# A masked graph attention kernel: which far blocks are turned by the vector engine, and where their mask stands

## What is computed

```
h = relu(layernorm(x))
cos = beta * (h @ h.T) / (norm2 @ norm2.T + 1e-07)
x = x + softmax(cos + (1 - adj) * -1e9, axis=1) @ h
h = relu(layernorm(x))
x = x + h @ W_self + (adj @ h / max(rowsum(adj), 1)) @ W_neigh
```

## Time and profile before

| | |
|---|---|
| median of 3 runs | 485.01 us (484.8 to 486.03) |
| profiled execution, its own time | 484.94 us |
| its span | 483.1 us |
| PE busy | 455.3 us (94%) |
| DVE, ACT, POOL busy | 294.9, 288.7, 264.0 us |
| TensorE clock granted | 1.000 |
| DMA | 59.68 MB, q1 (issued by SP) 49.42 MB |

### The profile page before, as it was taken

One profiled execution on the slowest core, in us unless ns is written; L12 is line 12 of the kernel. 1 busy time (PEld: TensorE's weight loads), 2 busy tenths in 40 slices (PEclk: granted clock), 3 DMA queues, 4 the chain that ended last, 5 costly groups with the idle time before them and its releaser, 6 DMA issues.

```text
span 483.1 us, 12207 instructions
## 1 busy us (share of the span) xinstructions
PE 455.3 (94%) x5096; PEld 380.3 (79%) x5096; DVE 294.9 (61%) x685; ACT 288.7 (60%) x437; POOL 264.0 (55%) x249
## 2 busy tenths in 40 slices
PE   0969999999999999999999998999999999999997
PEld 0837888788788887788777877887797888888886
DVE  6966656877676776768857777685776421022232
ACT  2999898767977768976797778677864000000000
POOL 3989777867958578775787578566562000000000
PEclk9999999999999999999999999999999999999999
DMA  8157879878799788997799598846500000000000
GB/s 245 28 65 153 173 141 215 196 167 163 158 232 211 156 194 148 239 208 162 137 216 222 87 203 199 188 69 98 79 3 2 6 23 20 23 23 23 23 23 22
DMA packets 45899, 59.68 MB, mean 124 GB/s; under 512 B 3600, under 2 KB 38672, under 8 KB 45840
## 3 DMA queue, kind: packets, MB, share of 16 engines
q1 hardware_dynamic: 35472, 49.42, 33.2%
q0 software_dynamic: 10368, 9.44, 24.6%
HBM read 78.25 MB, written 8.91 MB: 180 GB/s over the span
## 4 chain that ended last, share of the span: by engine, by line
PE 72%; ACT 12%; DVE 9%; issue 3%; POOL 2%; DMA 1%; SPq 0%; ACTq 0%; DVEq 0%; POOLq 0%
PE ps L1184 22%; PE ps L1058 13%; PE ps L1069 7%; ACT word L600 6%; PE ps L1167 5%; PE ps L1164 5%; PE ps L1166 5%; PE ps L1139 5%; PE ps L1142 4%; ACT ps L601 4%; PE ps L1141 4%; DVE far L866 3%; DVE word L834 1%; DVE adj_t L689 1%; DMA x_sb<-in_x_dram 1%
## 5 line engine op out<-in xcount | busy, mean ns | idle before, releaser
L453 POOL TENSOR_TENSOR near<-word,adj_t 128x1024 f32<-128x1024 f32 x72 | 151.8, 2108 | 82.9 <-DVE word L834 66.5
L600 ACT ACTIVATE word<-ps,small 128x512 f16<-128x512 f32 x144 | 136.2, 946 | 63.9 <-PE ps L1058 63.5
L834 DVE TENSOR_TENSOR word<-ps,word 128x512 f16<-128x512 f32 x144 | 105.9, 738 | 81.9 <-ACT ps L601 81.7
L1184 PE MATMUL ps<-table,adj_t 128*128 128x257 f16 x1024 | 115.0, 274 | 0.0
L1058 PE MATMUL ps<-unit_t 128*128 128x512 f16 x432 | 106.5, 379 | 6.7 <-DVE word L834 4.8
L1184 PEld LDWEIGHTS ps<-table,adj_t 128*128 128x128 fp8e4 x1024 | 100.0, 98 | 13.6
L601 ACT ACTIVATE ps<-ps,small 128x512 f32<-128x512 f32 x144 | 108.2, 751 | 0.0
L1164 PE MATMUL ps<-table,near 128*128 128x129 f16 x576 | 102.6, 219 | 2.2 <-POOL near L453 1.5
L1167 PE MATMUL ps<-table,near 128*128 128x129 f16 x576 | 102.9, 222 | 0.0
L1166 PE MATMUL ps<-table,near 128*128 128x128 f16 x576 | 102.6, 219 | 0.0
L1139 PE MATMUL ps<-table,far 128*128 128x129 f16 x448 | 80.0, 219 | 2.5 <-DVE far L866 2.0
(11 more groups left out here) (88 smaller groups left out, 472.7 us busy)
## 6 DMA issues: line engine op xcount, KB each, us to landing
stage<-in_adj_dram SPq DMA_DIRECT2D x56, 512.0 KB, 5.4
adj_t<-in_adj_dram POOLq DMA_DIRECT2D x72, 128.0 KB, 5.0
turned_blocks<-packed SPq DMA_DIRECT2D x13, 512.0 KB, 4.4
moved_words<-turned_blocks SPq DMA_DIRECT2D x52, 128.0 KB, 4.5
x_sb<-in_x_dram SPq DMA_DIRECT2D x4, 512.0 KB, 6.3
x_again<-in_x_dram SPq DMA_DIRECT2D x7, 256.0 KB, 5.8
out_dram<-x_sb SPq DMA_DIRECT2D x7, 256.0 KB, 2.3
far<-in_x_dram SPq DMA_DIRECT2D x1, 256.0 KB, 5.1
```

The costliest lines, as they stand in the source:

```text
L453: pool.tensor_tensor(ring(near, k), ring(word, k), adj_t[:, near_adj(k)], ALU.mult).then_inc(s_near, 1)
L600: act.activation(half(word16, k, c, 0, HIGH, TPS), score(k, c), ACT.Exp, bias=exp_bias, scale=exp_scale)
L834: dve.tensor_tensor(half(word16, k, c, 0, LOW, TPS), score(k, c), half(word16, k, c, 0, HIGH, TPS), ALU.subtract).then_inc(s_elo, 1)
L1184: return pe.matmul(ps[:, agg_bank(g, t), 0:TW], adj_t[:, at:at + P], tab(b), start=(b == 0), stop=(b == T - 1))
```

## The change

1. `moved_pairs`: a moved block is attended three entries after its own, where it was four. An entry that is second or third in its row group is neither moved nor, if it has a far block, a host. Moved blocks: 16 instead of 13, and PE transposes 40 instead of 43.
2. `mask_moved` for host k+1 stands in DVE's entry k between `spill` and `low_part(k+2, 1)`; only where an item follows `score(k+2, 1)` in the ring does it stand behind that `low_part`. It never stands ahead of `low_part(k+2, 0)` any more.
3. In PE's tail, `first_group([3], 8, 16)` moves ahead of the products of group 5, and two chunks of the next piece take its place.

```diff
-                    if k + 1 in GUEST and FAR_AT[k] is None:
-                        mask_moved(GUEST[k + 1])
                     if k + 2 < NP:
...
                     if k + 1 in NORMAL:
                         mask_far(k + 1)
+                    item_next = k + 3 < NP and RING[AT["score", k + 2, 1] + 1][0] != "score"
+                    if k + 1 in GUEST and not item_next:
+                        mask_moved(GUEST[k + 1])
                     if k + 2 < NP:
                         low_part(k + 2, 1)
-                    if k + 1 in GUEST and FAR_AT[k] is not None:
+                    if k + 1 in GUEST and item_next:
                         mask_moved(GUEST[k + 1])
...
             h2_transposes(5)
-            first_group([3], 0, 8)
+            first_group([3], 0, 16)
             h2_products(5, 0)
             h2_products(5, 1)
-            first_group([3], 8, 16)
+            first_group(ALL, 16, 18)
             h2_transposes(6)
-            first_group(ALL, 16, 20)
+            first_group(ALL, 18, 20)
             h2_transposes(7)
...
+    began = [i for i in range(1, len(order)) if order[i][0] != order[i - 1][0]]
+    busy = [i + d for i in began for d in (1, 2)]
     while k < len(order) and order[k][0] < 5:
-        if not far[k]:
+        if not far[k] or k in busy:
             k += 1
             continue
-        at = k + 4
+        at = k + 3
+        while far[at] and (at in busy or order[at][0] >= 5):
+            at += 1
         moved.append(k)
-        if order[at][0] >= 5:
-            at = min(i for i in range(at, len(order)) if not far[i])
         host[k] = at
         k = at
```

## The result

| | before | after |
|---|---|---|
| median | 485.01 us (7 runs, 484.62 to 486.22) | 481.75 us (7 runs, 480.29 to 483.49) |
| ratio | 1 | 0.9929 (0.991 to 0.9948) |
| profiled execution | 484.94 us | 481.54 us |

What follows compares the result with a forecast made beforehand. PE's own work plus its standing time was taken to bound the 70 entries. Terms -2.6 - 5.8 - 0.8 + 1.2 + 0.5 - 0.15 = -7.65 us took 484.94 to 477.3 us; range 474.0 to 482.0 us.

Steps and rivals of the forecast that it cites:

- transposes of three blocks: PE transposes three blocks fewer, at 0.88 us each read from start to start: 2.6 us less.
- first near product of group 4: PE's wait for `new_rows` in step 52 goes, since eight transposes now stand ahead of this product: 0.8 us less.
- gaps at hosts: PE's gaps before far products at hosts of moved blocks fall from 7.2 to 1.4 us: 5.8 us less.
- short steps 20, 34, 56: PE newly waits for POOL's near mask: about 0.5 us at 34 and 56, 0.2 at 20; 1.2 us added.
- trip through DRAM: Moved words must return sooner; tight only at blocks 19, 33 and 55 (11.0 us of room): 0.5 us added.
- tail: Aggregation matmuls fill PE's stand before group 5, but group 6 still awaits DVE's low half: 0.15 us less.
- It keeps up, with little to spare: ACT in short steps: 2.9 us an entry against 2.68 in one step and 3.56 in the next; no cost.
- over one step to spare: Loads behind the fetch in SP's queue (`load_far`) have over one step in hand, so no cost.
- The waits only move: Rival, chance 0.18: removed gaps return at other engines, DVE's second low half being 0.9 us later at every host; 481.4 us.
- The port: Rival, chance 0.10: POOL's tile conversion holds up the mask (L866), 0.3 to 0.5 us at some 6 hosts; 480 us.
- The slower rival: Chance 0.05: moved words return late from DRAM, holding DVE and the scores; 494 us with 16.3 us trips, decisive from 15.
- the five hosts with the mask behind the low half: Hosts 11, 25, 39, 51, 62, unchanged order: about 0.2 us gap in four, zero at 62; 0.8 us.

Runs made afterwards that it cites:

- one part alone: The new `moved_pairs` (16 moved blocks, three entries' distance) in the kernel before, with its old mask places and old tail: 485.66 us, ratio 1.0015.
- the other at least as much as both: The mask's new place in the kernel before, with its 13 moved blocks at four entries' distance and old tail: 479.84 us, ratio 0.9896.

## Why the prediction was right or wrong

The direction was right, and the measured time lies inside the range, near its end. The forecast itself was wrong: it gave 7.65 us where 3.4 came. Step by step, in us:

| step | predicted | measured |
|---|---|---|
| transposes of three blocks | -2.6 | -2.5 (PE's busy time) |
| first near product of group 4 | -0.8 | -0.8 (step 52 has no gap) |
| gaps at hosts | -5.8 | -0.3 (7.6 to 7.3) |
| short steps 20, 34, 56 | +1.2 | +0.4 (.14, .16, .14) |
| trip through DRAM | +0.5 | in the hosts: 51, and 0.16 at 48 |
| tail | -0.15 | -0.14 |
| sum | -7.65 | -3.4 |

*What failed* is the term of the gaps at the hosts (-5.8 us, measured -0.3), and in it one sentence: "Counted from the start S of the scores of the entry ahead: spill ends at S + 3.54 (87.83 - 84.29), mask until S + 4.75." It was read in entry 11, an ordinary entry, and applied to eleven hosts. For most of them it holds (32 above; 14 lost 0.22 to the port, and 45, which was costed apart, 0.39). For 22, 36, 48 and 58 the first low half comes at S + 3.8 to S + 4.4, since ACT has its conversion and, in just this entry of the group, the pair of L608 ahead of it. Two of the four then met POOL's conversion as well, and took 1.76 and 1.93 us. "It keeps up, with little to spare", said of ACT, was worked out from two exponentials an entry, without its conversions and without L608. Before, this cost nothing: no seventh entry was a host, and PE did not yet want the late low half. But it stood in the trace (S + 3.82 at step 35, S + 3.50 at step 47). The new list of hosts alone brings these gaps (7.1 us), the new place of the mask takes 1.0 to 2.8 us off them where the prediction had all of it, and moving L608 brings 4.1 us on the same chip. That is the experiments' answer.

*The trip through DRAM* was mis-sized in length and place. The 9.8 to 12.6 us took the median for each fetch's landing. Read to the landing of each block's last fetch, the thirteen trips of before took 8.3 to 14.6 us, and after the change they took 8.8 to 14.4 us and 17.1 at block 48. The prediction expected the cost at blocks 19, 33 and 55, which came back in 10.3, 11.5 and 10.4 us, in time. It came at block 48, where a store took 9.5 us to land.

The claim that the loads behind the fetch have "over one step to spare" fell as well: ACT's waits for tiles went from 1.5 to 5.7 us. They are of two kinds. In the first the transfer is long. The buffer was freed by ACT's conversion at 121.26, and the next load was issued at once and landed 6.6 us later:

```profile
120.20 1.06 ACT L575 ACTIVATE adj_t<-stage 128x1024 uint8<-128x1024 f32 x1
```

```profile
121.29 0.33 SPq L359 DMA_DIRECT2D stage<-in_adj_dram  x1
```

Over two short steps (2.68 and 4.05 us) that is late. In the second, the longest of all, the load stood in SP's queue. The buffer was free at 259.20, but SP held the fetch of block 48, whose store had not landed, and issued the load 3.7 us later, behind that fetch:

```profile
262.88 0.44 SPq L359 DMA_DIRECT2D stage<-in_adj_dram  x1
```

```profile
268.23 1.06 ACT L575 ACTIVATE adj_t<-stage 128x1024 uint8<-128x1024 f32 x1 [2.75 <-DMA stage<-in_adj_dram]
```

*The rivals.* "The waits only move" gave 481.4 us and is nearest, but not by its mechanism: it expected DVE's second low half to be late for PE, and those waits shrank (8.5 to 4.8 us). That its number is near is luck. "The port" is part of the truth: four of the 16 masks took 1.76 to 2.31 us (14, 22, 36, 51) and one 1.58 (28). It named the right pair, POOL's conversion beside L866. The Trainium skill (SBUF — State Buffer, SBUF: two separate sides) states that whichever of the two begins first holds the ports for its whole instruction. By that rule the mask at 132.17 should have stood until POOL's conversion ended at 132.86 and then have run its 1.2 us; that would be 134.07. It ended at 133.93, 1.07 us after POOL, and the trace agrees to 0.14 us. The slower rival came at one place only: 15 of the 16 trips stayed under 15 us, the longest of them by 0.6 us. In the two other profiles of the changed kernel two each were over 15 us (15.1 to 17.6), all at blocks 22 and 48.

*The other terms*: transposes, step 52 and tail held. The transposes were priced from start to start. The short steps cost a third of what was worked out; the wait is the one named, of PE's weight loads for POOL's near mask (1.7 us in four cases, before their lead over PE is taken off). Of the five hosts with the mask behind the low half, 11, 25 and 39 lost 0.05 us each where 0.2 was given, 62 nothing as forecast, and 51 its 2.18.

## What to carry to other kernels

An offset from the start of a step ("the operand is ready at S + 2.5") belongs to the step in which it was read. Before it is used for another place, read there what the other engines do in that step: their periodic work (here a conversion every second tile, and filler placed by the position in a group) decides. An in-order queue gives a moved instruction the lateness of all that is ahead of it, so when such an instruction is moved, move the filler with it. Read the place in the old trace too: a lateness that costs nothing yet is there to be seen. And try the parts of a change apart: here one part alone was worth nothing and the other at least as much as both, and a two-line shift of filler took the pair from 0.993 to 0.982 and 0.986 of before.

## What was not expected of the hardware

The same kernel's gaps moved by up to 2.1 us at one host from profile to profile, without a change in the program (36: 1.48, 1.88, 1.71; 58: .57, 2.21, 1.56; 51: 2.18, .05, 2.18). The runs of the changed kernel spread wider than before's (480.29 to 483.49 against 484.62 to 486.22 us in seven each). A single profile of such a kernel shows which places are late, and not by how much.

The landing time of a 512 KB store has a long tail: 2.9 us at the least, 5.4 in the median, 9.5 at most. Before, it was 3.0, 4.4 and 6.3. But that is no effect of the three more round trips: the kernel before with `second_h` later, with its 13, had 3.0, 5.4 and 9.2, and the new blocks alone, with 16, had 3.0, 4.8 and 7.9.
